# One unmasked copy on ScalarE, two masked products on GpSimd: attention outputs of a fused adaLN attention and int8 FFN kernel

## Chip, cores and metric

One core of a Trainium2 chip runs the whole kernel. The metric is the device time of one execution in microseconds. Engines are called by their names here: TensorE (PE in the profile), VectorE (DVE), ScalarE (ACT), GpSimd (POOL) and SyncE (SP).

## What is computed

The input is x with 8 batches of 512 tokens of 256 features, and a condition vector of 512 numbers per batch. The reference, cut to what matters:

```
x  = x * s1;  x = (x - mean) * rsqrt(var + eps)
q, k = heads(x @ Wq.T * q_dc), heads(x @ Wk.T * k_dc)        # 16 heads of 16
v_flat = x @ Wv.T * v_dc * s2
attn = softmax(q @ k.T * scale)                                # per head, 512 x 512
out  = (attn @ v) @ Ww.T * w_dc + v_flat @ Wu.T * u_dc
x + int8_matmul(quantise(out), quantise(rhs)) * scales          # 256 x 256
```

## The kernel before

The kernel is one program for each engine, with an order written out by hand and semaphores between the engines. A loop over the 8 batches t holds the order on every engine. TensorE's loop is cut into 8 steps i per batch. A step makes the scores of two rounds (`scores_of`), the products with the values of the two rounds before (`values_of`), and then a fill (`fill(t, i)`): a piece of the work of another batch (projections, transposes, the value and output products, the int8 product). A round is four heads by 128 keys; ScalarE makes the exponentials of a round in two instructions of 128x1024.

The products with the values are summed in one PSUM bank, `o_acc`, over the four rounds of a head group. The value tile `v_aug` has 32 columns for each head, 16 of values and 16 of ones, so a head's block of 32 partitions in `o_acc` holds outputs and sums of the exponentials. Four groups make up a batch, and two groups make a pair. The first group of a pair has its outputs in one half of each block, the second in the other half. `in_half` is a 128x2 tile of zeros and ones that says which half a partition lies in. The first group is saved by ScalarE (`save_first`): one copy times `in_half[:, 0:1]` to `o_raw`, one times `in_half[:, 1:2]` to `den`. The second group is added by VectorE (`add_second`), two instructions that read `o_acc`, multiply by the mask and add. Then VectorE turns the sums into factors (`invert`) and multiplies (`normalise`). TensorE's first product of the next group waits for the count `o_saved`, since the bank is the same.

Around these stand:

- ScalarE's order in a batch: the exponentials of 16 rounds, with `save_first` between the two rounds of steps 2 and 6, and the high parts of the next batch's q and k (`high_part`) in steps 3 and 4.
- GpSimd's order in a batch: the output weights (`demodulate_output`), the value weights of the next batch (`scale_values`), an inverse root for the batch after (`inverse_root`), four squares of the high parts (`square`), then a residual addition (`add_residual`) and an output store (`store`) of batch t - 2.
- VectorE's order in the middle of a batch: moments of x two batches ahead (`measure`), `add_skip`, `product`, `quantise` (largest value, scale, inverse, two products to y_q, one to y_int), the low parts 0 and 1 (`low_part`), `add_second`, `invert`, the low parts 2 and 3.
- The three banks of `work`: TensorE takes them in a fixed order and waits until VectorE has freed the bank of three uses ago. The bank of the norms (`norms`, line 1154) is the one that `low_part(a, 2)` frees.
- `shift`, a tile of the path with row maxima, written only when a bound on the scores is exceeded.

Of the kernel before, what the change touches and what calls it, by code (L numbers as in the profile page):

```python
# [6 lines left out]
F32R = mybir.dt.float32r  # L7
BF16 = mybir.dt.bfloat16
I32 = mybir.dt.int32
ALU = mybir.AluOpType  # L10
ACT = mybir.ActivationFunctionType
AX = mybir.AxisListType

P = 128
# [50 lines left out]
def adaln_ffn_kernel(nc, x, cond, wq, wk, wv, ww, wu, rhs, out):  # L65
    B, S, H = x.shape
    NH, D = 16, H // 16
# [36 lines left out]
    with ctx:  # L104
        def sb(name, shape, dt=F32):
            return ctx.enter_context(nc.sbuf_tensor(name, shape, dt))

        def sem(name):
            return ctx.enter_context(nc.semaphore(name))
# [33 lines left out]
        squares = sb("squares", [P, 4, S], BF16)  # L143
# [10 lines left out]
        k_stack = sb("k_stack", [P, 2, NP, S], F32R)  # L154

        row_max = sb("row_max", [P, KT, NH])
        shift = sb("shift", [NH, 2, S], F32R)

        probs = sb("probs", [P, RING, 4, S])


        in_half = sb("in_half", [P, 2])
        o_raw = sb("o_raw", [P, S])
        den = sb("den", [P, S])
        den_t = sb("den_t", [P, S])
# [32 lines left out]
        o_acc = ctx.enter_context(nc.psum_tensor("o_acc", [P, S], F32))  # L198
# [35 lines left out]
        shift_ready, last_stored = sem("shift_ready"), sem("last_stored")  # L234
        inverse_ready, demod_step = sem("inverse_ready"), sem("demod_step")
        st_ready, exp_done, pv_done, o_saved = sem("st_ready"), sem("exp_done"), sem("pv_done"), sem("o_saved")
        den_ready = sem("den_ready")
        o_normed, yq_ready, yqt_ready = sem("o_normed"), sem("yq_ready"), sem("yqt_ready")
        last_normed = sem("last_normed")
        res_ready, res_added = sem("res_ready"), sem("res_added")  # L240
# [2 lines left out]
        unit_ready, half_ready = sem("unit_ready"), sem("half_ready")  # L243
        spare = sem("spare")
# [133 lines left out]
        def _(pool):  # L378
# [18 lines left out]
            def inverse_root(a):  # L397

                pool.wait_ge(var_ready, a + 1)
                nc.gpsimd.tensor_tensor(rstd[:, :], var_eps[:, :], half[:, :].broadcast_to([P, KT]), ALU.pow  # L400
                                        ).then_inc(rstd_ready, 1)
# [38 lines left out]
            def square(a, n):  # L440
                pool.wait_ge(hi_ready, a * 4 + (n + 1))
                nc.gpsimd.tensor_tensor(squares[:, n, :], parts[:, n, 0, :], parts[:, n, 0, :], ALU.mult  # L442
                                        ).then_inc(squares_ready, 1)

            def add_residual(z):
                pool.wait_ge(res_loaded, z * 16 + 16)
                for i in range(1 if z == B - 1 else 2):
                    two = slice(2 * i, 2 * i + 2)
                    pool.wait_ge(res_ready, z * 2 + (i + 1))
                    nc.gpsimd.tensor_tensor(res[:, two, :], res[:, two, :], x_res[:, two, :], ALU.add  # L450
                                            ).then_inc(res_added, 1)

            def store(z):
                pool.wait_ge(res_added, z * 2 + 2)
                pool.sem_inc(spare, 1)
                nc.gpsimd.dma_start(out[z].rearrange("(k p) h -> p k h", p=P), res[:, :, :]).then_inc(pool_stored, 16)

            inverse_root(0)
            square(0, 0)
            square(0, 1)  # L460
# [4 lines left out]
            nc.gpsimd.memset(k_stack[:, 1, :, :].bitcast(F32), 1.0).then_inc(k_cleared, 1)  # L465
            nc.gpsimd.memset(q_stack[:, 1, :, :].bitcast(F32), 0.0).then_inc(q_cleared[1], 1)
            pool.wait_ge(ww_ready, 1)
            for t in range(B):
                a, y = t + 1, t - 2
                if y >= 0:  # L470

                    pool.wait_ge(work_ready, USE[("y", y, 1)] + 1)
                demodulate_output(t)
                if a < B:
                    pool.wait_ge(fold_ready, a)
                    pool.sem_inc(spare, 1)
                    scale_values(a)
                    if a + 1 < B:
                        inverse_root(a + 1)
                    for n in range(4):  # L480
                        square(a, n)
                if y >= 0:
                    add_residual(y)
                    store(y)
            add_residual(B - 2)
            store(B - 2)
            add_residual(B - 1)
# [2 lines left out]
        def _(act):  # L490
# [73 lines left out]
            def save_first(pair):  # L564

                act.wait_ge(pv_done, KT * (2 * pair + 1))
                if pair > 0:
                    act.wait_ge(o_normed, pair)
                nc.scalar.activation(o_raw[:, :], o_acc[:, :], ACT.Copy, scale=in_half[:, 0:1])
                nc.scalar.activation(den[:, :], o_acc[:, :], ACT.Copy, scale=in_half[:, 1:2]).then_inc(o_saved, 1)  # L570

            high_part(0, 0)
            high_part(0, 1)
# [25 lines left out]
            for t in range(B):  # L599
                a = t + 1  # L600
# [19 lines left out]
        def _(dve):  # L620
# [136 lines left out]
            def add_second(pair):  # L757

                dve.wait_ge(pv_done, KT * (2 * pair + 2))
                dve.wait_ge(o_saved, 2 * pair + 1)  # L760
                nc.vector.scalar_tensor_tensor(den[:, :], o_acc[:, :], in_half[:, 0:1], den[:, :], ALU.mult, ALU.add  # L761
                                               ).then_inc(den_ready, 1)
                nc.vector.scalar_tensor_tensor(o_raw[:, :], o_acc[:, :], in_half[:, 1:2], o_raw[:, :], ALU.mult, ALU.add
                                               ).then_inc(o_saved, 1)
# [206 lines left out]
            for t in range(B):  # L971
                a, z, y = t + 1, t - 1, t - 2
# [511 lines left out]
```

## Time and profile before

| | us |
|---|---|
| median of 3 runs | 422.87 (422.8 to 424.1) |
| the profiled execution | 425.1 |
| its span | 423.3 |
| busy: TensorE / VectorE / ScalarE / GpSimd | 406.2 / 278.1 / 295.9 / 106.3 |

The span is the time from the first to the last instruction in the trace; the profiled execution's own time is 1.8 us more. Busy shares are averages over stages with different limits. The granted TensorE clock is 0.98 in the mean.

### The profile page before, as it was taken

The page shows a single profiled execution, that of the slowest core. Times are in us where ns is not written, and L with a number is a line of the kernel's source. Part 1 is how long each engine was busy: PE and PEld are TensorE (multiplying, and loading weights), DVE is VectorE, ACT ScalarE, POOL GpSimd, SP SyncE. Part 2 cuts the span into 40 slices and gives each one's busy share as a digit, 9 for nine tenths or more (in the row PEclk, how much of TensorE's full clock was granted, in tenths as well). Part 3 has the DMA queues.
Part 4 walks back from the last instruction along what each step waited for, and adds up shares of the span by engine and source line. Part 5 has one row for each costly group of instructions (what it writes and reads, how often), then busy time and mean ns, then how long its engine had stood idle before and what let it go on. Part 6 is the DMA issues. An engine that isn't in the chain of part 4 may idle for free.

```text
span 423.3 us, 7589 instructions
## 1 busy us (share of the span) xinstructions
PE 406.2 (96%) x2542; PEld 216.5 (51%) x2542; DVE 278.1 (66%) x632; ACT 295.9 (70%) x343; POOL 106.3 (25%) x115
## 2 busy tenths in 40 slices
PE   8999899999999999999999999999999999999894
PEld 7785434454444554445544455454445544453363
DVE  7666387266865588477856788468847565648355
ACT  3526868858787787868787788677785878687811
POOL 7177023100320023502340042302350042011301
PEclk9869989999999999999999999999999999999999
DMA  5399527603684336622894246731782057502021
GB/s 170 109 139 133 129 43 131 129 9 99 119 130 112 99 67 133 165 82 75 135 151 108 100 96 129 181 101 39 135 174 62 38 125 136 142 0 101 3 98 50
DMA packets 29327, 44.19 MB, mean 104 GB/s; under 512 B 3880, under 2 KB 15144, under 8 KB 29256
## 3 DMA queue, kind: packets, MB, share of 16 engines
q1 hardware_dynamic: 27360, 38.84, 43.7%
q0 software_dynamic: 1040, 3.70, 2.6%
q10 hardware_dynamic: 880, 1.07, 1.4%
q8 instruction: 25, 0.41, 0.4%
q14 instruction: 22, 0.18, 0.2%
HBM read 14.17 MB, written 4.25 MB: 44 GB/s over the span
## 4 chain that ended last, share of the span: by engine, by line
PE 86%; DVE 7%; ACT 3%; issue 3%; POOL 0%; DVEq 0%; POOLq 0%
PE o_acc L1095 29%; PE scores L1081 19%; PE work L1146 12%; PE work L1123 10%; PE work L1206 6%; ACT probs L561 3%; PE work L1134 2%; PE scores L1123 2%; PE work L1249 1%; PE work L1058 1%; PE work L1235 1%; DVE q_stack L882 1%; PE work L1221 1%; PE work L1388 1%; DVE v_aug L702 1%
## 5 line engine op out<-in xcount | busy, mean ns | idle before, releaser
L561 ACT ACTIVATE probs<-scores 128x1024 f32<-128x1024 f32 x256 | 247.4, 1024 | 73.9 <-PE scores L1081 73.9
L1095 PE MATMUL o_acc<-probs,v_aug 128*32 128x512 f32 x1024 | 125.4, 605 | 0.3 <-issue 0.3
L1081 PE MATMUL scores<-q_stack,k_stack 50*128 50x512 f32 x512 | 96.7, 450 | 5.2 <-ACT probs L561 5.0
L1081 PEld LDWEIGHTS scores<-q_stack,k_stack 50*128 50x128 f32 x512 | 39.6, 184 | 77.4 <-ACT probs L561 61.4
L1095 PEld LDWEIGHTS o_acc<-probs,v_aug 128*32 128x32 f32 x1024 | 26.9, 110 | 60.9 <-issue 56.4
L1146 PE MATMUL work<-vs_w,x_t 128*128 128x512 f32 x192 | 51.6, 410 | 0.2 <-DVEq L962 0.2
L442 POOL TENSOR_TENSOR squares<-parts 128x512 bf16<-128x512 f32 x30 | 31.2, 1040 | 67.7 <-ACT parts L545 67.7
L702 DVE TENSOR_TENSOR v_aug<-work,rows 128x128 f32<-128x128 f32 x64 | 15.6, 286 | 45.1 <-PE work L1146 44.7
L1123 PE MATMUL work<-x_t,qk_w 128*128 128x512 f32 x168 | 43.0, 404 | 0.0
L1146 PEld LDWEIGHTS work<-vs_w,x_t 128*128 128x128 f32 x192 | 34.2, 188 | 15.8 <-issue 7.5
L450 POOL TENSOR_TENSOR res<-res,x_res 128x512 f32<-128x512 f32 x15 | 19.1, 1278 | 90.5 <-DVEq L848 90.5
L400 POOL TENSOR_TENSOR rstd<-var_eps,half 128x4 f32<-128x4 f32 x8 | 8.3, 1039 | 129.2 <-DVE var_eps L658 126.8
L1123 PEld LDWEIGHTS work<-x_t,qk_w 128*128 128x128 f32 x168 | 30.5, 188 | 11.5 <-issue 4.8
L1206 PE MATMUL work<-w_demod,o_n 128*128 128x256 f32 x112 | 27.9, 392 | 0.0
L1206 PEld LDWEIGHTS work<-w_demod,o_n 128*128 128x128 f32 x112 | 20.1, 189 | 7.3 <-issue 5.1
L761 DVE SCALAR_TENSOR_TENSOR den<-o_acc,in_half,den 128x512 f32<-128x512 f32 x16 | 12.0, 751 | 13.8 <-PE o_acc L1095 10.8
L426 POOL TENSOR_SCALAR wv_scaled<-wv_nat,cols 128x256 f32<-128x256 f32 x16 | 14.7, 924 | 14.5 <-DVEq L693 14.3
L646 DVE TENSOR_TENSOR x_sb<-x_sb,rows 128x1024 f32<-128x1024 f32 x7 | 8.9, 1274 | 14.3 <-DMA rows<-in_cond_dram 14.3
L798 DVE TENSOR_TENSOR y_q<-work,skip 128x512 f32<-128x512 f32 x16 | 11.0, 688 | 9.4 <-PE work L1206 8.5
L826 DVE TENSOR_SCALAR y_qt<-work 128x512 bf16<-128x512 f32 x14 | 9.7, 691 | 11.2 <-issue 9.5
L842 DVE SCALAR_TENSOR_TENSOR res<-work,y_scale,rhs_scale_row 128x256 f32<-128x256 f32 x28 | 12.2, 479 | 5.1 <-PE work L1249 3.6
L1134 PE MATMUL work<-wu_t,wv_scaled 128*128 128x256 f32 x64 | 15.4, 384 | 0.0
(168 smaller groups left out, 445.9 us busy)
## 6 DMA issues: line engine op xcount, KB each, us to landing
q_stack<-parts SPq DMA_DIRECT2D x96, 128.0 KB, 3.9
k_stack<-parts SPq DMA_DIRECT2D x92, 128.0 KB, 4.0
x_res<-in_x_dram SPq DMA_DIRECT2D x8, 512.0 KB, 4.6
x_sb<-in_x_dram SPq DMA_DIRECT2D x7, 512.0 KB, 5.1
out_dram<-res POOLq DMA_DIRECT2D x7, 512.0 KB, 4.6
rows<-rows_dram SPq DMA_DIRECT2D x7, 384.0 KB, 4.2
rows<-in_cond_dram SPq DMA_DIRECT2D x8, 128.0 KB, 4.9
x_sb<-in_x_dram SPq DMA_DIRECT2D x2, 256.0 KB, 4.0
```

Source lines behind the costliest of these rows:

```text
L426: last = nc.gpsimd.tensor_scalar(wv_scaled[:, c, :], wv_nat[:, c, :], cols[:, a, 2 + c:3 + c], None, ALU.mult)
L442: nc.gpsimd.tensor_tensor(squares[:, n, :], parts[:, n, 0, :], parts[:, n, 0, :], ALU.mult).then_inc(squares_ready, 1)
L450: nc.gpsimd.tensor_tensor(res[:, two, :], res[:, two, :], x_res[:, two, :], ALU.add).then_inc(res_added, 1)
L561: nc.scalar.activation(probs[:, r % RING, pair:pair + 2, :], scores[:, pair:pair + 2, :], ACT.Exp).then_inc(exp_done, 1)
L702: nc.vector.tensor_tensor(v_aug[:, k, :, e * D:(e + 1) * D].rearrange("p (n e j) d -> p n e j d", e=2, j=4)[:, :, e, :, :], both[:, 0:H].r ...
L842: last = nc.vector.scalar_tensor_tensor(res[:, q, :], bank[:, k * H:(k + 1) * H], y_scale[:, z % 2, q:q + 1], rhs_scale_row[:, :], ALU.mul ...
L1081: last = nc.tensor.matmul(scores[:, 2 * (u % 2) + e, :], k_stack[top:top + ROWS, t % 2, head, kt * P:(kt + 1) * P], q_stack[top:top + ROWS ...
L1095: last = nc.tensor.matmul(o_acc[DV * j:DV * (j + 1), :], v_aug[:, kt, 4 * g + j, :], probs[:, r % RING, 2 * (j % 2) + j // 2, :], start=(k ...
L1123: last = nc.tensor.matmul(bank, lhs, right, start=(n == 0), stop=(n == len(operands) - 1))
L1134: last = nc.tensor.matmul(bank[:, hc * H:(hc + 1) * H], wv_scaled[:, c, hc * P:(hc + 1) * P], wu_t[:, c, :], start=(c == 0), stop=(c == HC ...
L1146: last = nc.tensor.matmul(bank, lhs, right, start=(n == 0), stop=(n == len(operands) - 1))
L1206: last = nc.tensor.matmul(bank[:, k * H:(k + 1) * H], o_n[:, c, tok], w_demod[:, z % 2, c, :], start=(c == 0), stop=(c == HC - 1))
```

## The change

ScalarE now copies the first group of a pair once, without a mask, into a new tile `o_first`, waits for its own copy and raises `o_saved`. GpSimd makes `den` and `o_raw` from that copy (`part_first`), and VectorE's second addition waits for it (`first_parted`). `part_first` of a batch's first pair stands between the inverse root and the squares, that of the second pair behind the store. The tile `shift` is laid over the tile of the squares.

```
-        shift = sb("shift", [NH, 2, S], F32R)
+        shift = squares[0:NH, :, :].rearrange("h (j n) t -> h j (n t)", j=2).bitcast(F32R)
...
+        o_first = sb("o_first", [P, S])
...
+            def part_first(pair):
+
+                pool.wait_ge(first_taken, pair + 1)
+                if pair > 0:
+                    pool.wait_ge(o_normed, pair)
+                nc.gpsimd.tensor_scalar(den[:, :], o_first[:, :], in_half[:, 1:2], None, ALU.mult)
+                nc.gpsimd.tensor_scalar(o_raw[:, :], o_first[:, :], in_half[:, 0:1], None, ALU.mult
+                                        ).then_inc(first_parted, 1)
...
             pool.wait_ge(ww_ready, 1)
+            pool.wait_ge(half_ready, 1)
+            pool.sem_inc(spare, 1)
...
                     if a + 1 < B:
                         inverse_root(a + 1)
+                part_first(2 * t)
+                if a < B:
                     for n in range(4):
                         square(a, n)
                 if y >= 0:
                     add_residual(y)
                     store(y)
+                part_first(2 * t + 1)
...
                 act.wait_ge(pv_done, KT * (2 * pair + 1))
                 if pair > 0:
-                    act.wait_ge(o_normed, pair)
-                nc.scalar.activation(o_raw[:, :], o_acc[:, :], ACT.Copy, scale=in_half[:, 0:1])
-                nc.scalar.activation(den[:, :], o_acc[:, :], ACT.Copy, scale=in_half[:, 1:2]).then_inc(o_saved, 1)
+                    act.wait_ge(first_parted, pair)
+                    act.sem_inc(spare, 1)
+                nc.scalar.activation(o_first[:, :], o_acc[:, :], ACT.Copy).then_inc(first_taken, 1)
+                act.wait_ge(first_taken, pair + 1)
+                act.sem_inc(o_saved, 1)
...
                 dve.wait_ge(pv_done, KT * (2 * pair + 2))
-                dve.wait_ge(o_saved, 2 * pair + 1)
+                dve.wait_ge(first_parted, pair + 1)
```

## Rows read from the trace of the kernel before

**Rows 1.** The page, chain that ended last, by engine.

```profile
PE 86%; DVE 7%; ACT 3%; issue 3%; POOL 0%; DVEq 0%; POOLq 0%
```

**Rows 2.** Timeline at saves: start, length, engine, line, names, count [idle before <- releaser].

```profile
49.64 0.69 ACT L569 ACTIVATE o_raw<-o_acc,in_half 128x512 f32<-128x512 f32 x1 [0.18 <-PE o_acc L1095]
...
50.79 3.76 ACT L561 ACTIVATE probs<-scores 128x1024 f32<-128x1024 f32 x4
...
51.87 0.49 PE L1081 MATMUL scores<-q_stack,k_stack 50*128 50x512 f32 x2 [1.05 <-ACT probs L561]
...
77.42 0.50 PE L1081 MATMUL scores<-q_stack,k_stack 50*128 50x512 f32 x2 [0.20 <-ACT probs L561]
...
397.93 0.49 PE L1081 MATMUL scores<-q_stack,k_stack 50*128 50x512 f32 x2 [0.65 <-ACT probs L561]
```

**Rows 3.** Chain in order of time: start, length, what; batch 2's second save, and elsewhere.

```profile
170.40 0.78 PE scores L1081 x4
...
181.72 0.66 PE scores L1081 x4
```

**Rows 4.** Timeline around the norms, batch 1 and then batch 3.

```profile
115.00 0.12 PEld L1154 LDWEIGHTS work<-squares,head_ones 128*32 128x32 bf16 x4 [0.30 <-POOL squares L442]
...
207.32 0.75 DVE L682 SCALAR_TENSOR_TENSOR parts<-work,cols,parts 128x512 fp32r<-128x512 f32 x1
...
208.24 0.13 PEld L1154 LDWEIGHTS work<-squares,head_ones 128*32 128x32 bf16 x4 [0.77 <-POOL squares L442]
```

**Rows 5.** Groups by line and form: count | busy us, mean ns | idle before.

```profile
L569 ACT ACTIVATE o_raw<-o_acc,in_half 128x512 f32<-128x512 f32 x16 | 11.0, 687 | 3.7 <-PE o_acc L1095 3.7
...
L545 ACT ACTIVATE parts<-scores 128x512 fp32r<-128x512 f32 x2 | 1.2, 597 | 2.6 <-PE scores L1123 2.6
...
L426 POOL TENSOR_SCALAR wv_scaled<-wv_nat,cols 128x256 f32<-128x256 f32 x16 | 14.7, 924 | 14.5 <-DVEq L693 14.3
```

**Rows 6.** Timeline of ScalarE in the setup, a copy behind its own wait.

```profile
29.54 1.09 ACT L586 ACTIVATE o_n<-work 8x512 f32<-8x512 f32 x2 [0.22 <-PE work L1058]
...
30.25 0.37 ACT L586 ACTIVATE o_n<-work 8x256 f32<-8x256 f32 x1
```

**Rows 7.** Timeline of GpSimd and VectorE, batch 3.

```profile
197.12 1.04 POOL L400 TENSOR_TENSOR rstd<-var_eps,half 128x4 f32<-128x4 f32 x1 [20.61 <-DVE var_eps L658]
...
199.09 1.04 POOL L442 TENSOR_TENSOR squares<-parts 128x512 bf16<-128x512 f32 x1 [0.93 <-ACT parts L545]
...
199.69 0.47 DVE L807 TENSOR_SCALAR y_scale<-amax 128x2 f32<-128x2 f32 x1
...
200.39 1.46 DVE L811 TENSOR_SCALAR y_q<-y_q,y_inv 128x256 f32<-128x256 f32 x2
200.40 1.04 POOL L442 TENSOR_TENSOR squares<-parts 128x512 bf16<-128x512 f32 x1 [0.27 <-ACT parts L545]
...
201.89 0.43 DVE L815 TENSOR_SCALAR y_int<-y_q 128x512 bf16<-128x512 f32 x1
202.23 0.75 DVE L682 SCALAR_TENSOR_TENSOR parts<-work,cols,parts 128x512 fp32r<-128x512 f32 x1
```

**Rows 8.** Timeline, output store of GpSimd and VectorE's second addition.

```profile
172.35 0.88 POOL L456 DMA_DIRECT2D out_dram<-res  x1 [0.66 <-POOL res L450]
...
178.60 0.75 DVE L761 SCALAR_TENSOR_TENSOR den<-o_acc,in_half,den 128x512 f32<-128x512 f32 x1 [0.31 <-DVE y_qt L826]
```

**Rows 9.** Single lines of VectorE: duration in ns, min/median/max, first and last start.

```profile
L807 DVE TENSOR_SCALAR y_scale<-amax x16: 169/170/759, 106.0 to 414.8; 128x2 f32<-128x2 f32 x16
...
L811 DVE TENSOR_SCALAR y_q<-y_q,y_inv x28: 340/350/1197, 106.4 to 391.3; 128x256 f32<-128x256 f32 x28
```

**Rows 10.** Timeline in the setup, GpSimd's value weights beside VectorE.

```profile
26.68 0.93 POOL L426 TENSOR_SCALAR wv_scaled<-wv_nat,cols 128x256 f32<-128x256 f32 x1
26.82 0.35 DVE L658 TENSOR_SCALAR var_eps<-mv 128x4 f32<-128x4 f32 x1
27.09 0.68 DVE L950 TENSOR_TENSOR squares<-parts 128x512 bf16<-128x512 f32 x1
```

More of the change, by code:

```diff
@@ L236, in adaln_ffn_kernel @@
         st_ready, exp_done, pv_done, o_saved = sem("st_ready"), sem("exp_done"), sem("pv_done"), sem("o_saved")
-        den_ready = sem("den_ready")
+        den_ready, first_taken, first_parted = sem("den_ready"), sem("first_taken"), sem("first_parted")
         o_normed, yq_ready, yqt_ready = sem("o_normed"), sem("yq_ready"), sem("yqt_ready")
```

## The prediction

> **What bounds the kernel now.** I read the page first: in the chain that ended last 86% is TensorE [rows 1]. So only time that TensorE stands idle, or in which its order is held up, can be won or lost. Then I looked for what holds TensorE near the code that changes, in the timeline. Two places matter.
>
> The first is behind each first-group save. ScalarE starts the first copy at 49.64 in batch 0, and the next exponentials only at 50.79, 1.15 us later; TensorE then waits 1.05 us for the first of them [rows 2]. At the other saves fills cover more. The waits that I find are: 1.05 at batch 0's first save; 0.20 or 0.19 at three saves (batch 0's second, both of batch 1; the first of the three is in [rows 2]); in batches 2 to 6, at the second save, a score group that takes 0.78 where 0.66 is usual, so about 0.11, five times [rows 3]; and 0.65 at the last save [rows 2].
>
> The second is behind VectorE. The norms of the next batch take the bank that VectorE frees with its third low part. In batches 2 to 5 that low part ends at 207.32 + 0.75 = 208.07, and TensorE loads the norms' weights at 208.24, with 0.77 of idle weight load before them; in batches 0, 1 and 6 the idle is 0.30, so the weights are loaded some 0.47 ahead there [rows 4]. So in four batches VectorE has no slack at all, and what delays it between its work on y_q and that low part goes to TensorE in full: there VectorE's instructions follow one another.
>
> **The change, part by part.**
>
> ScalarE: two copies with a scale from a tile, 0.687 each or a little less, become one without it. The nearest row is the same form from PSUM without a tile's scale, 0.597 [rows 5]. The new code waits for its own copy before it raises the count, and the next instruction is behind that wait. The same pattern is in the setup: a 512-element copy starts at 29.54, ends by 0.60 later, and the one behind the own wait starts at 30.25, a gap of 0.11 [rows 6]. So the exponentials start 0.60 + 0.11 = 0.71 after the copy instead of 1.15: 0.44 earlier. The bounds are 0.05 (if the waits in front of the copy and of the exponential, which the engine now meets idle, cost most of it) and 0.55 (no gap at all). What TensorE gets back is the smaller of that and its wait: 0.44 at the first save, 0.44 at the last, 0.20 + 0.19 + 0.19, and 5 x 0.11 = 0.55. Sum 2.0 us; by the bounds 0.5 (ten places of 0.05) to 2.2. The remaining saves have no wait and give nothing. TensorE's own wait for the saved bank comes over 2 us later and was not late.
>
> GpSimd gets 32 products of 128x512 with a scale from a tile. The trace has this operation only at 128x256: 0.924 [rows 5]. At twice the elements it cannot be under 0.924, nor over twice that, 1.85. A square with two inputs and 512 elements takes only 1.04 [rows 7], 2.0 ns an element with all that is fixed in it; by that 256 more elements of one input should cost half of 0.52 to the whole of it, 1.18 to 1.44. I take the lower, 1.2, because one tile is read in place of two. A pair of them takes 2.4 (1.9 to 3.7).
>
> Is that late for VectorE's second addition? For the first pair of a batch they stand behind the inverse root, which ends at 197.12 + 1.04 = 198.16 [rows 7]. So they end near 200.5, at worst 201.9; the addition comes behind two low parts of about 0.75, the first of which starts at 202.23. For the second pair they stand behind the store, whose issue ends at 172.35 + 0.88 = 173.23: done by 175.6, at worst 176.9, and the addition starts at 178.60 [rows 8]. Queued behind them on GpSimd are the next batch's output weights and value weights, which move 2.4 to 3.7 us back; on SP the load of the rows waits for the output weights, but also for the first value product of the batch after, which comes later. In the last batch the second pair's products stand before the residual addition of batch 6, so that addition, its store and SP's last residual load go back by about as much; the load is wanted only by the last addition of the kernel, and the store by the products before it, which stand behind the whole of VectorE's last quantisation. The waits added cost nothing there. The shift buffer is only written on the path with row maxima, which is not taken; moving it is free. The extra wait for the halves at the start is long satisfied.
>
> What is not free is the company. VectorE's products from SBUF to SBUF wait while GpSimd works. In batch 3, squares run on GpSimd at 199.09 to 200.13 and at 200.40 to 201.44; VectorE's scale, usually 0.17, takes 0.47, and its two y_q products, usually 0.35 each or 0.61 together, take 1.46 [rows 7, 9]. So about 1.15 us per batch of such blocking is in the time already. The change puts the two new products just in front (198.13 to 200.5) and pushes the squares to about 200.5 to 202.5. How long does a product with a tile's scale block? There is one sighting: GpSimd starts such a product of 256 elements at 26.68 for 0.93, VectorE's scale starts at 26.82 and ends at 27.17, 0.18 longer than such a short one usually takes [rows 9], and an SBUF to SBUF operation of VectorE behind it takes its plain 0.68 from 27.09 [rows 10]. So it blocked 0.5 us at most, not 0.93. For 512 elements I take 0.7 (0.5 to 0.96).
>
> With that and 1.2, in batch 3: the second product starts at 199.3 and blocks until 200.0; the scale ends there, the first y_q product runs at 200.2, the first square starts at 200.45 and blocks the second until 201.5, it ends at 201.7; the second square blocks the y_int product until 202.5, which ends at 202.8 in place of 202.32. VectorE is then 0.5 later. But with 1.35 us or more for a product the y_q products get in before the squares, only y_int meets one or none, and VectorE is 0.2 to 1.0 *earlier*; in an unlucky order it is 0.9 later. Earlier is worth nothing to TensorE, as it was only just waiting. I take 0.2 later over these, in four batches: + 0.8 us (0 to 3.6). Batches 0 and 1 have some slack, and in batch 6 there is no inverse root, the products run before the y_q work.
>
> The sum: - 2.0 + 0.8 = - 1.2 us. The profiled execution took 425.1 (span 423.3, 1.8 around it) and would take 423.9; it lies 2.2 above the median of the three runs, 422.87, from which the same shift gives **421.7**.
>
> The Trainium skill (SBUF — State Buffer, "SBUF: two separate sides") says that the port pair that both engines share is an exclusive lock, kept for the whole instruction. By the squares of batch 3 the trace agrees; by the product at 26.68 it does not. By the rule the sum would be the one of the first rival below. The same skill (GPSIMD Engine Reference, "Engine selection") calls one-input operations roughly line-rate there, which speaks for the lower end of the price of a product; the sum does not use it.
>
> **Rivals.**
>
> *The new products block VectorE for their whole length.* With 1.2 us each, in batch 3: the scale is held until 200.5; the squares follow at 200.5 and 201.6 and each takes its turn against the y_q products and y_int, which ends at 203.4, 1.05 late. Four batches make 4.2, batch 1 with its 0.5 of slack about 1.3: + 5.5, less 2.0 is + 3.5, **426.4**. With 1.85 each it is 2.2 late per batch and the total + 9, 432. For it: the squares do just this. Against it: [rows 10]. It decides from about 0.5 us of lateness in each of four batches on, where the gain is used up. This is the case on the other side. Chance 0.20.
>
> *The gain does not come.* The own wait and the two waits in front eat the 0.44, or the waits of TensorE reappear at the next exponentials. With 0.5 of gain and 0.8 of loss: **423.2**. Chance 0.14.
>
> *GpSimd becomes the bound of the second addition.* Needs over 2.6 us per product in the second pairs; nothing near it in the rows. It would be slower, about 424 and more. Chance 0.02.
>
> My forecast has 0.64. Its own range is 420.6 (2.2 gained, nothing lost) to 424.5 (3.6 lost, 2.0 gained).
>
> **How the numbers follow.** What a measurement of this kernel can tell from no change is about 0.3%, 1.27 us. Inside my forecast, I give 0.39 of the 0.64 to VectorE not being later or hardly (420.6 to 421.6: faster), 0.20 to within 0.3%, 0.05 to slower. The second case is within (0.12; 0.02 slower). The first and third rivals are slower, 0.20 and 0.02. Rounded: faster 0.39, same 0.33, slower 0.28. For 8 in 10 the range runs from 420.4 to 427.2: it holds the forecast's cases, the second rival and the cheaper half of the first.
>
> **What would show it.** ScalarE's copy at 0.60 and exponentials some 0.7 behind its start; TensorE's wait of 1.05 in batch 0 down to about 0.6 and those of 0.19 gone; GpSimd's products at 1.2 each and back to back. The step on which all hangs is VectorE from the scale to y_int in batches 1 to 5: the low part of batch 3 starts at 202.1 to 202.8 by my forecast, from 203.3 on by the first rival, and the norms follow the third low part at once. What would make the prediction wrong: products much longer than 1.2 us that also block for all their length, or a pattern in which VectorE never gets a turn between four GpSimd instructions in a row; that would cost over 2 us in each of five batches.

## The result: 0.5% faster

| | before | after |
|---|---|---|
| median, us | 422.95 (14 runs) | 420.98 (14 runs; 419.77 to 422.36) |
| ratio | | 0.995, 95% interval 0.9933 to 0.9967 |
| the profiled execution / its span | 425.1 / 423.3 | 420.03 / 418.2 |

Two of the 14 runs of before took 496.91 and 1182.48 us and don't enter the ratio; the others lie between 422.14 and 426.78, with a median of 422.84.

The gain is 1.97 us by the medians (1.86 without those two runs), where 1.2 was forecast (421.7). The spans differ by 5.1, which is too much: the profiled execution of before carried a chance event, told in the first experiment. A second profile of that kernel has a span of 420.1, so like for like it is 1.9, and the comparisons below use that second profile.

The page of the profile after, busy time by engine:

```profile
PE 401.9 (96%) x2542; PEld 215.0 (51%) x2542; DVE 275.2 (66%) x632; ACT 287.0 (69%) x327; POOL 157.2 (38%) x147
```

ScalarE has 8.9 us less than before, GpSimd 50.9 more: 32 products. Its groups by line and form (count | busy us, mean ns | idle before):

```profile
L444 POOL TENSOR_TENSOR squares<-parts 128x512 bf16<-128x512 f32 x30 | 31.6, 1062 | 27.6 <-ACT parts L561 27.6
L465 POOL TENSOR_SCALAR den<-o_first,in_half 128x512 f32<-128x512 f32 x16 | 25.4, 1589 | 52.0 <-ACT o_first L586 51.8
L466 POOL TENSOR_SCALAR o_raw<-o_first,in_half 128x512 f32<-128x512 f32 x16 | 25.4, 1589 | 0.0
```

A product takes 1.56 to 1.59 us, not 1.2. The timeline at the first save of batch 0 and at the last save, which answers to [rows 2]:

```profile
48.29 0.60 ACT L586 ACTIVATE o_first<-o_acc 128x512 f32<-128x512 f32 x1 [0.17 <-PE o_acc L1113]
...
49.06 3.77 ACT L577 ACTIVATE probs<-scores 128x1024 f32<-128x1024 f32 x4 [0.17 <-PE scores L1099]
50.14 0.50 PE L1099 MATMUL scores<-q_stack,k_stack 50*128 50x512 f32 x2 [0.67 <-ACT probs L577]
...
66.64 0.40 PE L1172 MATMUL work<-squares,head_ones 128*32 128x512 bf16 x4 [0.78 <-DVEq L705]
...
391.03 0.60 ACT L586 ACTIVATE o_first<-o_acc 128x512 f32<-128x512 f32 x1 [0.75 <-PE o_acc L1113]
391.80 3.77 ACT L577 ACTIVATE probs<-scores 128x1024 f32<-128x1024 f32 x4 [0.18 <-ACT o_first L586]
392.88 0.50 PE L1099 MATMUL scores<-q_stack,k_stack 50*128 50x512 f32 x2 [0.38 <-ACT probs L577]
```

The exponentials start 0.77 behind the start of the copy (0.71 forecast, 1.15 before), and TensorE's wait is 0.67 instead of 1.05. The score group behind the second save of batch 2, in the chain in order of time, takes its plain 0.66 where [rows 3] has 0.78:

```profile
171.26 0.66 PE scores L1099 x4
```

Now the step on which the forecast hung: GpSimd, VectorE and the norms' weights in batch 3, timeline, to be held against [rows 4] and [rows 7]:

```profile
192.91 1.04 POOL L402 TENSOR_TENSOR rstd<-var_eps,half 128x4 f32<-128x4 f32 x1 [17.48 <-DVE var_eps L676]
193.95 1.56 POOL L465 TENSOR_SCALAR den<-o_first,in_half 128x512 f32<-128x512 f32 x1
195.50 1.56 POOL L466 TENSOR_SCALAR o_raw<-o_first,in_half 128x512 f32<-128x512 f32 x1
197.03 2.20 POOL L444 TENSOR_TENSOR squares<-parts 128x512 bf16<-128x512 f32 x2
...
195.48 0.22 DVE L825 TENSOR_SCALAR y_scale<-amax 128x2 f32<-128x2 f32 x1
...
195.93 0.67 DVE L829 TENSOR_SCALAR y_q<-y_q,y_inv 128x256 f32<-128x256 f32 x2
196.63 0.71 DVE L833 TENSOR_SCALAR y_int<-y_q 128x512 bf16<-128x512 f32 x1
197.26 0.73 DVE L700 SCALAR_TENSOR_TENSOR parts<-work,cols,parts 128x512 fp32r<-128x512 f32 x1
...
203.48 0.12 PEld L1172 LDWEIGHTS work<-squares,head_ones 128*32 128x32 bf16 x4 [0.30 <-POOL squares L444]
```

Both products to y_q run in 0.67 us while GpSimd is inside its second product (195.50 to 197.06), and the squares come only when they are done. Only y_int, 0.71 instead of its plain 0.43, still runs beside a square. The low part starts 4.35 behind the inverse root's start; before it was 202.23 - 197.12 = 5.11. The norms' weights are loaded ahead again (idle 0.30, it was 0.77). So VectorE is 0.76 earlier here, not 0.2 later.

### The profile page after: what moved, and what is told of

It reads as the page before. It is cut to its first block, busy times and chain, and to the rows that moved or that the text cites. A ratio compares the mean times of both kernels' runs of the same rounds, so it can differ in the third digit from the quotient of the medians.

```text
span 418.2 us, 7636 instructions
## 1 busy us (share of the span) xinstructions
PE 401.9 (96%) x2542; PEld 215.0 (51%) x2542; DVE 275.2 (66%) x632; ACT 287.0 (69%) x327; POOL 157.2 (38%) x147
## 4 chain that ended last, share of the span: by engine, by line
PE 80%; DVE 7%; DMA 6%; issue 2%; SPq 2%; ACT 1%; ACTq 0%; DVEq 0%
PE o_acc L1113 26%; PE scores L1099 18%; PE work L1164 10%; PE work L1141 9%; PE work L1224 6%; PE work L1152 3%; DMA rows_dram<-o_n 2%; PE scores L1141 2%; DMA y_q<-in_L_cond_k_weight_dram 1%; PE work L1267 1%; SPq L298 1%; ACT probs L577 1%; DMA rows<-in_cond_dram 1%; DMA x_res<-in_L_cond_u_weight_dram 1%; PE work L1253 1%
## 5 line engine op out<-in xcount | busy, mean ns | idle before, releaser
L1113 PE MATMUL o_acc<-probs,v_aug 128*32 128x512 f32 x1024 | 123.1, 598 | 0.0
L465 POOL TENSOR_SCALAR den<-o_first,in_half 128x512 f32<-128x512 f32 x16 | 25.4, 1589 | 52.0 <-ACT o_first L586 51.8
L466 POOL TENSOR_SCALAR o_raw<-o_first,in_half 128x512 f32<-128x512 f32 x16 | 25.4, 1589 | 0.0
```

The costliest lines, as they stand in the source:

```text
L465: nc.gpsimd.tensor_scalar(den[:, :], o_first[:, :], in_half[:, 1:2], None, ALU.mult)
L466: nc.gpsimd.tensor_scalar(o_raw[:, :], o_first[:, :], in_half[:, 0:1], None, ALU.mult).then_inc(first_parted, 1)
L1113: last = nc.tensor.matmul(o_acc[DV * j:DV * (j + 1), :], v_aug[:, kt, 4 * g + j, :], probs[:, r % RING, 2 * (j % 2) + j // 2, :], start=(k ...
```

## The experiments

To see below one per cent in single profiles, I read the starts of the 16 first-group copies of ScalarE in each timeline and took their differences. Interval 1 runs from the first copy to the second. From interval 2 on they repeat to 0.03 us between profiles, except where a chance event falls into one (as in the 11th of after, 23.63 instead of 23.32, which the table leaves out). Odd intervals run from a batch's first save to its second, even ones to the next batch; "end" is from the last copy to the end of the span.

| kernel | 2 | 3 | 4 | 5 | 6 | 7 | 8 | 13 | 14 | end |
|---|---|---|---|---|---|---|---|---|---|---|
| before again | 22.63 | 23.43 | 23.00 | 23.43 | 22.99 | 23.42 | 22.99 | 23.35 | 21.79 | 27.56 |
| after | 22.36 | 23.07 | 22.71 | 23.32 | 22.89 | 23.32 | 22.88 | 23.32 | 21.69 | 27.17 |
| products beside | 22.64 | 23.35 | 22.99 | 23.35 | 23.01 | 23.35 | 22.99 | 23.35 | 21.81 | 27.61 |
| no products | 22.94 | 23.15 | 22.71 | 23.39 | 22.88 | 23.38 | 22.88 | 23.32 | 21.68 | 27.17 |
| early products | 22.35 | 23.16 | 22.71 | 23.41 | 22.90 | 23.40 | 22.89 | 23.34 | 21.68 | 27.20 |
| no own wait, again | 22.16 | 22.88 | 22.51 | 23.34 | 22.87 | 23.32 | 22.88 | 23.33 | 21.69 | 26.90 |
| two inputs | 22.36 | 24.49 | 23.09 | 24.13 | 22.88 | 24.41 | 22.88 | 23.33 | 21.68 | 27.15 |

(In the profile of "no products" TensorE's granted clock is at 0.50, the lower of its two levels, from 71 to 73 us, and 16 value products take 3.11 us there instead of 1.92. The 22.94 comes in the interval just behind that; that the fall caused it is not shown.)

**The kernel before, once more.** No edit.

> The kernel before, unchanged, timed against itself. Theory of the occupation (ScalarE's shorter save gives TensorE back about 2 us): ratio 1.000, and the wait of 1.05 us at batch 0's first save is there again. Rival, the clock: in the profile of before, the 16 value products behind that wait took 3.59 us in place of 1.92, 1.67 more. If that belongs to the wait, the second profile shows it too; if it is chance, the second profile has a span about 1.5 to 3 us shorter at the same time otherwise.

Measured: 423.74 us, ratio to before 1.0015 (0.9994 to 1.0036), span 420.1. Timeline:

```profile
50.33 0.51 PE L1081 MATMUL scores<-q_stack,k_stack 50*128 50x512 f32 x2 [1.06 <-ACT probs L561]
...
66.64 0.40 PE L1154 MATMUL work<-squares,head_ones 128*32 128x512 bf16 x4 [0.70 <-DVEq L687]
```

The wait of 1.06 behind the first save is there, but a second one stands behind it at 66.64 in this execution that the first profile didn't have: the norms of batch 0 wait for VectorE. In the first profile TensorE came there later than VectorE, since its value products in front took 3.52 us instead of 1.85. The chain of the first profile, in order of time:

```profile
53.29 3.52 PE o_acc L1095 x16
```

TensorE's granted clock there is 0.50, the lower level, from 54 to 56 us; it had stood idle for 1.05 and 0.42 us just before. In the second profile the same two waits are followed by no fall. So the slow products are chance in the sense that they come in one execution and not in the other.

**The wait covered.** Eight small products of TensorE in front of the transposes of the right features (`right_features`), so that TensorE is busy where it waited.

```
             bank = claim("rhs", 0, 0)
+            keep_clock(bank, 8)
```

> The kernel before, with 8 extra products of 128x128 on TensorE in batch 0, step 2, into a bank that is overwritten behind them; they fill 0.9 of the 1.05 us in which TensorE waits for the exponentials. Theory of the occupation: TensorE waits for ScalarE all the same, ratio 1.000 (within 0.001). Rival, the clock: the idle time is what makes the granted clock fall; with it covered the 1.7 us come back and the time is 1.0 to 1.7 us less, ratio 0.996 to 0.998.

Measured: 423.79 us, ratio 1.0008 (0.9992 to 1.0024). The idle time is gone (a row at 48.63, in which each small product counts twice, has 16 and takes 2.05 us, and the scores follow at 51.05 with no wait) and the median is the same. So in the median the 1.05 us of idle time cost nothing through the clock. It is not shown that such a wait never brings the fall: one of the two profiles of before, and that of the kernel with three products below, have one right behind it, worth about 1.6 us. The profile of this run has no fall, but two other delays, of 1.5 and 1.6 us, in intervals 2 and 6.

**ScalarE's part alone.** The changed kernel without GpSimd's products; VectorE's additions read `o_first` in place of both halves, so the masks of the first group are left out.

```
-                nc.gpsimd.tensor_scalar(den[:, :], o_first[:, :], in_half[:, 1:2], None, ALU.mult)
-                nc.gpsimd.tensor_scalar(o_raw[:, :], ...).then_inc(first_parted, 1)
+                pool.sem_inc(first_parted, 1)
```

> The changed kernel without GpSimd's 32 products: VectorE adds the second group to the unmasked copy, so the masks of the first group are left out of the computation. ScalarE is as in the changed kernel. Theory of the occupation: the gain of the changed kernel, 2.0 us, plus what the products cost in batch 0, where VectorE is 0.16 later and the norms wait 0.78: 2.1 to 2.8 less than before. Rival, that the products help (they move the squares behind VectorE's products on y_q, low part 0.76 earlier in batch 3): without them the four waits of 0.07 return and the time is 0.1 to 0.5 more than that of the changed kernel.

Measured: 422.25 us, ratio 0.9961 (0.9941 to 0.9982), span 421.2 with the clock event named above. The fourth and the later even intervals are those of after; the odd ones of batches 2 to 5 are 23.38 to 23.40 where after has 23.32. The median is only 0.9 us under that of before (2.1 to 2.8 was expected), but the interval of its ratio holds that of the changed kernel, 0.995, so the time alone doesn't tell the two apart. By the intervals the ScalarE side brings what it brings without the products, and the products cost nothing: they give 0.07 us in each of those batches.

**GpSimd's part alone.** The kernel before, and beside it 32 products of the same form from a settled tile into a spare one.

```
+                settled = wv_nat[:, :, :].rearrange("p c o -> p (c o)")
+                for n in range(2):
+                    nc.gpsimd.tensor_scalar(o_spare[:, n, :], settled, in_half[:, 1 - n:2 - n], None, ALU.mult
+                                            ).then_inc(pool_setup, 1)
```

> The kernel before, with ScalarE's two masked copies, and with 32 products of the changed kernel's form added on GpSimd at the same places, from a settled tile into spare tiles that nobody reads. It has their cost alone (and the shift buffer laid over the squares). Theory of the occupation with a short hold of the port (0.7 of 1.56 us by batches 1 and 3 of the changed kernel): ratio 0.999 to 1.001; products 1.56 us each, VectorE's low part of batch 3 no later than before. Rival, whole-length blocking: 3 to 9 us slower, ratio 1.008 or more. Rival, that moving the squares back is what gains: 1 us or more faster.

Measured: 422.39 us, ratio 0.9982 (0.9961 to 1.0004), span 419.9. Timeline of batch 3:

```profile
195.17 3.11 POOL L467 TENSOR_SCALAR o_spare<-wv_nat,in_half 128x512 f32<-128x512 f32 x2
...
197.15 0.66 DVE L828 TENSOR_SCALAR y_q<-y_q,y_inv 128x256 f32<-128x256 f32 x2
...
198.25 2.20 POOL L443 TENSOR_TENSOR squares<-parts 128x512 bf16<-128x512 f32 x2
```

No loss at all: the first rival (5.5 us of loss) is refuted, and so is the forecast's own 0.8. The odd intervals of batches 1 to 5 are 23.35 against 23.43: a gain of 0.08 each, in a kernel whose ScalarE is unchanged. Five times that is 0.4 us; the ratio, a little under the 0.999 to 1.001 expected, is in keeping with it.

**Products ahead of the inverse root.**

```
+                part_first(2 * t)
+                if a < B:
                     if a + 1 < B:
                         inverse_root(a + 1)
-                part_first(2 * t)
-                if a < B:
                     for n in range(4):
                         square(a, n)
```

> The changed kernel with the products of a batch's first pair ahead of the inverse root instead of behind it. The theory (products of 1.56 us hold VectorE for about 0.7 us each at their start, and where they stand they push the squares behind the products to y_q, so that TensorE's waits for the norms of batches 2 to 5 are 0.07 to 0.08 shorter) expects: the products now run some 17 us earlier, beside other work of VectorE that nobody waits for; squares and products to y_q meet again as in the kernel before, the third low part is late by the old amount, and the odd intervals between the first-group copies of batches 2 to 5 go from 23.32 back to 23.39. In the whole +0.3 us (0 to +0.5) against the changed kernel, a ratio to the kernel before of 0.995 to 0.996. The rival, that the products where they stand delay VectorE, expects 0.8 us less than the changed kernel, a ratio of 0.993.

Measured: 421.04 us, ratio 0.9939 (0.9918 to 0.9959), which lies between the two expectations and reaches into both; the time can't tell 0.3 us, the intervals can. Timeline of batch 3:

```profile
195.83 1.04 POOL L444 TENSOR_TENSOR squares<-parts 128x512 bf16<-128x512 f32 x1 [0.88 <-ACT parts L561]
197.13 1.04 POOL L444 TENSOR_TENSOR squares<-parts 128x512 bf16<-128x512 f32 x1 [0.26 <-ACT parts L561]
...
197.13 1.46 DVE L829 TENSOR_SCALAR y_q<-y_q,y_inv 128x256 f32<-128x256 f32 x2
...
204.98 0.13 PEld L1172 LDWEIGHTS work<-squares,head_ones 128*32 128x32 bf16 x4 [0.77 <-POOL squares L444]
```

With the products gone from this place the squares meet y_q again, the pair takes 1.46 again, the norms' weights wait 0.77 again, and the odd intervals are back at 23.40 to 23.41. So what the products gave is that they keep the squares away from y_q.

**No own wait of ScalarE.** The copy raises `o_saved` itself; GpSimd waits for `o_saved`.

```
-                nc.scalar.activation(o_first[:, :], o_acc[:, :], ACT.Copy).then_inc(first_taken, 1)
-                act.wait_ge(first_taken, pair + 1)
-                act.sem_inc(o_saved, 1)
+                nc.scalar.activation(o_first[:, :], o_acc[:, :], ACT.Copy).then_inc(o_saved, 1)
```

> The changed kernel in which the copy itself raises o_saved, so that ScalarE doesn't wait for its own copy before the exponentials; GpSimd waits for o_saved. The theory (the gap of 0.11 us behind the own wait lies in front of the exponentials, and TensorE gets it back wherever it still waits) expects exponentials 0.60 behind the start of the copy instead of 0.71 to 0.77, TensorE's waits of 0.67 in batch 0 and 0.4 at the last save 0.1 shorter, and 0.1 in each of some four to nine places: -0.2 to -0.9 us against the changed kernel. The rival, that the 16 saves give back nothing more because the scores' order bounds it now, expects 0.0.

Measured: 420.36 us, ratio 0.992 (0.9902 to 0.9939). Because that stood close to the changed kernel, both were run again side by side.

> The changed kernel once more, on the same chip and in the same rounds as the next run, so that the two can be told apart. Expected: ratio to before 0.994 to 0.996, a time 1.7 to 2.5 us under that of before; the first-group copies of batches 2 to 5 at intervals of 23.32 and 22.88 again.

Measured: 420.59 us (419.9 to 421.12), ratio 0.9945 (0.9927 to 0.9963), span 418.7.

> The version without ScalarE's own wait once more, beside the changed kernel. If the copy-to-exponential time of 0.50 us instead of 0.77 (seen in its profile) is worth what the intervals between the copies show (0.2 each in three intervals of batches 0 and 1 and 0.24 at the end, some 0.3 behind the first copy, nothing in batches 2 to 6), it is 0.8 to 1.1 us under the changed kernel, ratio to before 0.992 to 0.993. If the difference seen so far was only scatter, 0 to 0.3 us.

Measured: 419.52 us (418.94 to 421.71), ratio 0.9932 (0.9909 to 0.9955), span 417.1. Timeline of its first save:

```profile
48.21 0.60 ACT L586 ACTIVATE o_first<-o_acc 128x512 f32<-128x512 f32 x1 [0.17 <-PE o_acc L1111]
48.70 3.77 ACT L577 ACTIVATE probs<-scores 128x1024 f32<-128x1024 f32 x4
...
49.77 0.49 PE L1097 MATMUL scores<-q_stack,k_stack 50*128 50x512 f32 x2 [0.38 <-ACT probs L577]
```

Without the wait the exponentials start 0.49 behind the copy, even before it ends, where the changed kernel has 0.77. The own wait costs 0.28 us each time, not the gap of 0.11 that [rows 6] show. Intervals 2, 3 and 4 are shorter by 0.2 each and the end by 0.27; from batch 2 on nothing is left to gain. By the medians it is 0.6 (against the runs of the result, in other rounds) and 1.1 us under the changed kernel; the two intervals of the ratios overlap, so the times alone don't settle it, the intervals between the copies do (0.2 + 0.2 + 0.2 + 0.27 = 0.87).

**Both edits.** Products early, and no own wait.

> Both of these edits in one kernel: products of the first pair ahead of the inverse root, and no own wait of ScalarE. If the two are independent the time is the sum: -0.6 to +0.3 us against the changed kernel. If the products' place matters as the forecast had it (VectorE later behind them) it is the fastest of all, ratio 0.990 to 0.992.

Measured: 419.78 us (419.22 to 422.57), ratio 0.9925 (0.9897 to 0.9953). The odd intervals of batches 2 to 5 are 23.39 to 23.41, as with the early products; the second and the fourth are 22.15 and 22.53, as without the own wait, and the third is 22.96, 0.08 more, which the early products add. So the two effects are independent, and the early products are no help.

**Products from two tiles.** The same results, from the copy times a 128x512 mask in place of a column of two numbers.

```
-                nc.gpsimd.tensor_scalar(den[:, :], o_first[:, :], in_half[:, 1:2], None, ALU.mult)
+                nc.gpsimd.tensor_tensor(den[:, :], o_first[:, :], mask[:, 1, :], ALU.mult)
```

> The changed kernel with each of the 32 products of GpSimd made from two tiles (the copy times a 128x512 mask tile made once in the setup) in place of a tile and a scale from a 128x1 column; same results. The theory (a one-input product holds the port that VectorE needs for only about 0.7 of its 1.56 us, a two-input one, like the squares, for its whole length) expects products of 1.04 to 1.3 us each that hold VectorE till they end, as the squares do: in batches 2 to 5 y_int ends about 1 us later than in the kernel before, and with no slack there that is +3 to +5 us against the changed kernel, and 0.5 to 1 in batch 1: a ratio to before of 1.003 to 1.008. The rival, that the kind of product makes no difference to VectorE and only its length counts, expects the changed kernel's time or less (-0.5 to 0).

Measured: 429.7 us, ratio 1.0132 (1.01 to 1.0163), span 428.3. That is 8.7 us more than the changed kernel by the medians of different rounds, and 7.7 by the two ratios; 3 to 5 was expected for batches 2 to 5 and up to 1 more for batch 1. Timeline of batch 3:

```profile
199.88 1.29 POOL L466 TENSOR_TENSOR den<-o_first,mask 128x512 f32<-128x512 f32 x1
201.14 1.27 POOL L467 TENSOR_TENSOR o_raw<-o_first,mask 128x512 f32<-128x512 f32 x1
202.38 2.08 POOL L445 TENSOR_TENSOR squares<-parts 128x512 bf16<-128x512 f32 x2
...
201.43 1.01 DVE L829 TENSOR_SCALAR y_scale<-amax 128x2 f32<-128x2 f32 x1
...
202.67 1.93 DVE L833 TENSOR_SCALAR y_q<-y_q,y_inv 128x256 f32<-128x256 f32 x2
204.64 0.43 DVE L837 TENSOR_SCALAR y_int<-y_q 128x512 bf16<-128x512 f32 x1
204.98 0.75 DVE L704 SCALAR_TENSOR_TENSOR parts<-work,cols,parts 128x512 fp32r<-128x512 f32 x1
```

y_scale, usually 0.17, starts 0.29 into a product and ends 0.03 behind its end; then the squares hold y_q. The low part starts 6.12 behind the inverse root, 1.77 later than in the changed kernel, though each product is 0.3 *shorter*. The kind of the product decides, not its length. The intervals add it up: against after, the odd ones of batches 1 to 5 are 1.4, 0.8, 1.1, 0.8 and 1.0 longer, the fourth 0.4, and in batch 0 the second save stands 22.07 behind the addition that waits for a transfer (shown below), where after has 19.32: 2.7. Sum 8.2. Batches 2 to 5 make 3.7 of it, as expected; what the expectation missed is batch 1 with 1.8 and above all batch 0 with 2.7, where the same products meet VectorE's quantisation of the right features (its scale takes 0.94 us instead of 0.36). The prediction's first rival was right about two-input products and wrong about those of the changed kernel. No run has a one-input product without a column of scales, so whether the number of inputs or the instruction itself makes the difference is not shown.

**Products from two tiles, early.** Both edits.

> The products made from two tiles, as in the run two_input_products, and the first pair's ahead of the inverse root. The theory (the 8.7 us that two inputs cost come from two products of 1.28 us that hold VectorE to their end, just in front of the squares, where VectorE makes y_scale, y_q and y_int) expects that they vanish with the place: the products then run some 17 us earlier beside nothing that is on the path, so the time is that of early_products, ratio to before 0.994 to 0.997. The rival, that the mask tile or the products of the second pairs cost the time, expects 4 us or more of it to stay, a ratio of 1.004 to 1.013.

Measured: 422.12 us (420.73 to 426.62), ratio 0.9984 (0.9948 to 1.0019). By the medians 7.6 of the 8.7 us are gone with the place, by the ratios 6.3 of 7.7, and the odd intervals of batches 2 to 5 are 23.39 to 23.41. The ratio is a little above what was expected; its 95% interval reaches into it. One interval between copies, the fourth, is 23.08 instead of 22.71. It is 23.09 with the two-input products in their old place too, so it doesn't hang on the place of the first pairs' products; the second pairs' and the mask tile are the same in both runs, and which of them it is stays open.

**Three products per pair.**

```
+                nc.gpsimd.tensor_scalar(o_twice[:, :], o_first[:, :], in_half[:, 1:2], None, ALU.mult).then_inc(pool_setup, 1)
                 nc.gpsimd.tensor_scalar(den[:, :], o_first[:, :], in_half[:, 1:2], None, ALU.mult)
```

> The changed kernel with a third one-input product per pair, ahead of the two, into a tile that nobody reads. The theory (a one-input product holds VectorE for about 0.7 of its 1.56 us, and pushes the squares back) expects for the first pairs: the last product starts 1.56 us later, at about rstd + 4.1, and meets the second y_q product or y_int; the two first squares move to rstd + 5.7, behind y_int, where the low parts run. VectorE loses up to one more hold of 0.7 and wins back what the squares took: the third low part -0.3 to +0.5 us against the changed kernel in batches 2 to 5, in the whole -0.2 to +2 us (the slack is 0.08 now), a ratio to before of 0.994 to 1.000. By whole-length holds each batch would be 1.6 us later from batch 1 on, +6 to +8 us.

Measured: 421.68 us, ratio 0.9953 (0.9925 to 0.9981). Timeline of batch 3:

```profile
193.13 1.04 POOL L403 TENSOR_TENSOR rstd<-var_eps,half 128x4 f32<-128x4 f32 x1 [15.80 <-DVE var_eps L678]
...
197.26 1.72 POOL L468 TENSOR_SCALAR o_raw<-o_first,in_half 128x512 f32<-128x512 f32 x1
...
197.48 0.73 DVE L702 SCALAR_TENSOR_TENSOR parts<-work,cols,parts 128x512 fp32r<-128x512 f32 x1
```

The low part is 4.35 behind the inverse root, to the digit as with two; the odd intervals of batches 2 to 5 are 23.33. Another 1.56 us of GpSimd's time in front of the squares costs those batches nothing. In batch 0 the second save is 19.91 behind the addition, 0.6 more than in after, but not through VectorE: its third low part starts 12.99 behind the addition in both. It is TensorE that comes later, at the lower level of its clock (granted 0.50 from 52 to 54 us), and finds nothing to wait for at the norms. TensorE's timeline:

```profile
51.26 3.51 PE L1115 MATMUL o_acc<-probs,v_aug 128*32 128x512 f32 x16
...
66.94 0.40 PE L1174 MATMUL work<-squares,head_ones 128*32 128x512 bf16 x4
```

## Why the prediction was right, and by what it missed

The direction and the mechanism on ScalarE were right; 421.7 was forecast and 420.98 measured. The step on which the forecast hung, VectorE, came out with the other sign, and the number is near in part by luck. By the steps:

**ScalarE gives TensorE 2.0 us back: right in sum by luck, not place by place.** From the table, before again against after: intervals 2, 3 and 4 give 0.27, 0.28 and 0.29 (0.36 in the third, less the 0.08 of the squares), where 0.20, 0.19 and 0.19 were taken; the even intervals from 6 on give 0.10 to 0.12 five times (0.11 taken); the end 0.39 (0.44 taken); the odd ones of batches 2 to 6 give 0.02 to 0.03 each beside the 0.08 of the squares (the 11th can't be read), which is at the edge of the scatter and was taken as nothing. Sum 0.84 + 0.54 + 0.39 + 0.15 = 1.9. The rule that TensorE gets back the smaller of ScalarE's gain and the wait seen was too low: behind batch 0's second save, where the wait was 0.20, the changed kernel gains 0.27 and the one without the own wait another 0.20. What passes on the rest is not shown.

**The 0.44 at batch 0's first save: wrong, it gave nothing.** The second save of batch 0 doesn't follow the first, but VectorE's addition of the condition's rows, which waits for a transfer. Timeline rows of after and, below, of its second run: that addition and the second save:

```profile
52.70 1.23 DVE L664 TENSOR_TENSOR x_sb<-x_sb,rows 128x1024 f32<-128x1024 f32 x1 [3.79 <-DMA rows<-in_cond_dram]
...
72.02 0.60 ACT L586 ACTIVATE o_first<-o_acc 128x512 f32<-128x512 f32 x1 [0.74 <-PE o_acc L1113]
```

```profile
53.34 1.22 DVE L664 TENSOR_TENSOR x_sb<-x_sb,rows 128x1024 f32<-128x1024 f32 x1 [4.50 <-DMA rows<-in_cond_dram]
...
72.67 0.60 ACT L586 ACTIVATE o_first<-o_acc 128x512 f32<-128x512 f32 x1 [0.74 <-PE o_acc L1113]
```

| kernel | addition starts | second save | difference |
|---|---|---|---|
| before again | 52.64 | 71.92 | 19.28 |
| products beside | 52.78 | 72.03 | 19.25 |
| after | 52.70 | 72.02 | 19.32 |
| after again | 53.34 | 72.67 | 19.33 |
| no own wait | 53.47 | 72.81 | 19.34 |
| no own wait, again | 52.73 | 72.08 | 19.35 |
| early products | 53.48 | 72.87 | 19.39 |

The difference is 19.25 to 19.39 whatever ScalarE does at 48 us: there VectorE, behind that transfer, leads, and TensorE, which has less to wait for at 50 us, waits for VectorE at 66.64 all the same ([0.78 <-DVEq L705], 0.70 before). The forecast read one idle gap in the profile and took it as the bound; that profile, with the slow products behind the gap, hid the next wait.

**GpSimd's product: 1.2 forecast, 1.56 to 1.59 measured.** Inside the bounds of 0.92 to 1.85, above the guess of 1.18 to 1.44. It mattered, through the next step.

**VectorE 0.2 later in four batches, + 0.8 us: this is the step that failed, in sign; the runs show about - 0.4.** It was worked out with products of 1.2 us, after which squares and y_q collide. The text itself says that from 1.35 us on the y_q products get in before the squares and VectorE is 0.2 to 1.0 earlier. That case came: 0.76 earlier in batch 3 (4.35 behind the inverse root against 5.11). "Earlier is worth nothing" was wrong too: it is worth 0.08 us in each of batches 1 to 5, 0.4 together, shown by the products beside (23.35 against 23.43) and by the early products (back at 23.40).

**How long a product holds VectorE: 0.7 forecast; right that it is not the whole length.** In batch 3 y_q starts 0.43 into the product and runs plainly. In batch 1 the two meet head on (timeline):

```profile
103.75 1.79 POOL L466 TENSOR_SCALAR o_raw<-o_first,in_half 128x512 f32<-128x512 f32 x1
...
103.15 1.47 DVE L829 TENSOR_SCALAR y_q<-y_q,y_inv 128x256 f32<-128x256 f32 x2
104.65 0.43 DVE L833 TENSOR_SCALAR y_int<-y_q 128x512 bf16<-128x512 f32 x1
```

The pair takes 0.8 more than its plain 0.67 and ends 0.87 into the product; y_int then runs in its plain 0.43 inside it. So the hold is 0.43 us or less in one case and up to 0.87 less the second product's own 0.35 in the other. In the same batch y_scale, at 102.56, takes 0.35 instead of 0.17 beside the product that starts at 102.21; less its own 0.17 that ends 0.53 behind the product's start. About 0.5 is my estimate from these; the hold itself is in no row, and the product in the head-on case takes 1.79 instead of 1.56, so GpSimd loses there too.

The Trainium skill (SBUF — State Buffer, "SBUF: two separate sides") gives the shared pair to one engine for the whole instruction. By the 1.01 us of y_scale beside a two-input product the traces agree; by y_q and y_int, which wait for squares (y_q 1.46 in [rows 7], y_int 0.71 in the result's timeline) and yet run plainly inside one-input products, they do not, and the measurement decides. The Trainium skill (GPSIMD Engine Reference, "Engine selection") has one-input work roughly at line rate and two-input work slower; here the one-input product with a column of scales takes 1.56 us and the two-input one 1.28, the other way round.

**The second rival (the gain does not come)**, 423.2 us, would be a ratio of about 1.00; 0.9933 to 0.9967 was measured, which refutes it. **The third (GpSimd as the bound)** did not come: even with three products per pair, 4.8 us in place of 3.2, the time stays the same within its interval.

The sum by what was measured: 1.9 of ScalarE and 0.4 of GpSimd make 2.3, where the forecast had 2.0 - 0.8 = 1.2; the medians give 1.97, and 2.24 in the second comparison.

The fastest version here is the changed kernel without ScalarE's own wait: 420.36 and 419.52 us in two comparisons, ratios 0.992 and 0.9932. With the early products as well (419.78, 0.9925) it can't be told apart from that.

## What to carry to other kernels

A wait seen before an engine is a gain only if nothing else stands ready behind it: look for the next wait on the same path in a second profile, and compare the distances between repeated instructions in two profiles of each kernel rather than the spans, which here scatter by 3 to 4 us. In this kernel the work on GpSimd beside VectorE was priced by its kind (a tile and a column of scales, or two tiles) and its place, not by its length: the same results cost some 8 us more from two tiles, and most of that went when the products were moved to another place. Let the instruction itself raise the count that others wait for; ScalarE's wait for its own copy cost 0.28 us each time, and 0.87 us of the kernel's time.

## What the runs showed of the hardware that I had not expected

- ScalarE starts the next exponential 0.11 us before the copy in front of it has ended (48.70 against 48.21 + 0.60), so a wait for its own result costs that overlap as well: 0.28, where the gap in the trace of after shows 0.17.
- Two-input products of GpSimd (128x512, 1.28 us) hold VectorE's work from SBUF to SBUF to their end (y_scale beside one took 1.01 us instead of 0.17); one-input products with a column of scales (1.56 us) do so for about 0.5 us, by the estimate above.
- The granted clock differs from execution to execution in the setup. Windows of TensorE, from 10 to 20 us, in after and in its second run (length; busy and count; granted clock; DMA share; GB/s):

```profile
10.00:20.00 10.00, 8.92 (x53) 0.83 0.35 110
```

```profile
10.00:20.00 10.00, 9.60 (x47) 0.66 0.37 119
```

The transfer of the condition's rows is waited for until 52.70 and 53.34 in them; the second run without the own wait has 1.00 and 52.73. The six profiles with 0.66 there have the addition at 53.34 to 53.76; of the eight with 0.83 or 1.00 seven have it at 52.42 to 52.87. The eighth, the first profile of before, has 53.37, and 0.66 from 20 to 30 us. That it is the clock which makes the addition late is an inference from this, not tested.
